# Second attention of a fused two-layer kernel: the transposed scores, the turned maxima and the heads' normalisation are placed later within the pairs of heads

## The chip, the cores and the metric

One core of a Trainium2 chip runs the whole program as one launch. The metric is the device time of one execution in microseconds (us), as a median over several. TensorE (PE), VectorE (DVE), ScalarE (ACT), GpSimd (POOL) and the queue of transfers (SP) each run their own instruction stream and meet only at semaphores.

## The reference, cut to what matters

The program computes two transformer layers on four sequences of 512 tokens and width 256. Only the second layer's attention is touched:

```python
q = (x @ Wq).reshape(b, s, 16, 16); k = ...; v = ...   # 16 heads of width 16
scores = einsum('bqhd,bkhd->bhqk', q, k) * 0.25
p = softmax(scores)
o = einsum('bhqk,bkhd->bqhd', p, v).reshape(b, s, e)
x = x + o @ Wo + bo
```

The feed-forward part that comes before it (mixture of experts) and the one after it (ternary weights, GELU) are not changed, but the second attention overlaps with both at its ends.

## The kernel before, in words

`TT` is 4 (tiles of 128 tokens), `BATCHES` 4, `PAIRS` 8: the 16 heads go through in pairs. `pair_step(b, n, ...)` is written once for each engine. It has 8 **places** `i` = 0 to 7, and in each place every engine does its share of several pairs at different stages. The order in each engine's stream is fixed by these places, written out by hand:

- *Scores.* At place `i` TensorE computes scores of pair `n`: head `h = i // 4`, query tile `t = i % 4`, 512 keys (line 1689, called S1 below). The two heads of a pair are stacked in `qst` and `kst`: head 0 in the upper 64 partitions, head 1 in the lower 64 (`rows = slice(64 * h, 64 * h + 64)`). VectorE takes the negative maximum over keys of each (line 1005) into `nm1`. There are three PSUM banks for these scores.
- *Turned maxima.* When all eight maxima of a pair are there, TensorE transposes them (line 1714, four matmuls against `ident`, into PSUM bank 7) at place 1 of the next pair, and VectorE adds them to the queries (line 1014, `qsm`).
- *Transposed scores.* TensorE computes scores with keys on the partitions (line 1702, called ST below) from `kst` and `qsm`, eight per pair, numbered `e` = 0 to 7, with head `e // 4`. They begin at place 4 of the next pair and end at place 3 of the one after it. ScalarE takes the exponential of each (line 1338) into `pT1`. There are two PSUM banks for them, so ST number `e` waits for exponential `e - 2`.
- *Values.* Two pairs together are multiplied with `v1` (line 1728, four 32-column tiles side by side; the trace shows two records for each matmul, eight in one place), at places 5 and 7 of odd pairs and 1 and 3 of even ones. ScalarE copies the sum to `oT1` at place 4 of an even pair, TensorE turns it back (line 1742, PSUM bank 7) at place 6.
- *Normalisation of the heads.* VectorE divides by the sums (lines 1032 and 1034, reciprocal and `otok`) at place 7 of the even pair, right after that place's maximum. The turned maxima of an odd pair go into the same PSUM bank 7 and wait for it (`o1_normed`), and so does the turning of `otok` (line 1640) that feeds the output projection (line 1647).

At set places TensorE also does 128-row work of other stages: projections of queries and keys (lines 1416 to 1418, places (n, i) = (0, 5), (1, 3), (4, 5), (5, 3)), of values ((2, 5), (3, 0)), transposes in pairs 3 and 4 (line 1640 at (3, 2) and (3, 4), line 1634), and the output projection at (6, 5) and (7, 3). After such a projection ScalarE has two copies to make (lines 1278 and 1324). Sequence 0 lacks the projections of (0, 5), (1, 3), (2, 5), (3, 0) and all of the output projection; the last one lacks those of (4, 5) and (5, 3).

The queue SP loads the stacked heads, ring of four (`STACK_RING`): the load for pair `k` waits until the last ST of pair `k - 4` is done (line 422), and between pairs 3 and 4 and after pair 7 it also moves the projected heads through DRAM (line 413).

After the last sequence come four pair steps without new scores (`TAIL1`), which are interleaved with the first steps of the last feed-forward: VectorE makes ternary weights after steps 0 and 1 (lines 1043 to 1055), and hidden block `f` = 0 comes after step 2, blocks 1 to 8 after step 3:

```python
MLP_AFTER = {2: (0,), 3: (1, 2, 3, 4, 5, 6, 7, 8)}
for n in range(TAIL1):
    pair_step(BATCHES, n, False, True, False)
    ...
    for f in MLP_AFTER.get(n, ()):
        mlp_step(0, f, True, False, True)
```

In `mlp_step(0, 0)` TensorE computes block 0 (line 1837), ScalarE its GELU (line 1390) and a copy (line 1395), and VectorE waits for that copy and subtracts (line 1097). In tail step 3 TensorE turns `otok` at places 0 and 2 (line 1640) and ScalarE keeps it (line 1349).

Of the kernel before, what the change touches and what calls it, by code (L numbers as in the profile page):

```python
# [23 lines left out]
TT = SEQ // P  # L24
# [52 lines left out]
def build(nc, dram, out):  # L77
    with ExitStack() as ctx:
# [261 lines left out]

        MLP_AFTER = {2: (0,), 3: (1, 2, 3, 4, 5, 6, 7, 8)}
        TAIL1 = 4
        hidden_used = lambda f: -1 if f == 0 else f - 2 if f >= 2 else None
        hidden_split = lambda f: f if f < HT else None
        hidden_age = lambda f: 2 if f < 2 else 3
# [304 lines left out]
        def _(dve):  # L650
# [343 lines left out]
            def pair_step(b, n, new, old, following, places=range(2 * TT)):  # L994

                kb, kq, i_next = b * PAIRS, b * (PAIRS // 2), b + BATCHES + 1
                valid = lambda m: new if m >= 0 else old
                for i in places:
                    if new:

                        p = 2 * TT * n + i
                        h, t = i // TT, i % TT
                        dve.wait_ge(s1_ready, kb * 2 * TT + p + 1)
                        col = 64 * h + MAX_ROW
                        V.tensor_reduce(nm1[:, n % 2, t, col:col + 1], ps[:, 1 + s1_slot(p), :], AX.X, ALU.max,  # L1005
                                        negate=True).then_inc(s1_max, 1)
                    if i == 1 and valid(n - 1):

                        m = n - 1
                        k = kb + m  # L1010
                        dve.wait_ge(m_turned, k + 1)
                        if old or m >= 2:
                            dve.wait_ge(st_ready, (k - 1) * 2 * TT)
                        V.tensor_tensor(qsm[:, m % 2, :], ps[:, 7, :], qst[:, m % STACK_RING, :], ALU.add
                                        ).then_inc(qsm_ready, 1)
                    if new and n == 1 and i % 2 == 1:

                        if i == 1:
                            if not following:
                                dve.wait_ge(raw_used, raw_before(2))  # L1020
                            dve.wait_ge(xn_ready, i_next * TT)
                            V.memset(spare[:, 1:2], 0.0)
                        norm_stats(i_next, (b + 1) % BATCHES, (i // 2,))
                    if i == 2 * TT - 1 and n % 2 == 0 and valid((n - 4) // 2):

                        u = (n - 4) // 2
                        c0 = (u % (PAIRS // 2)) * 4 * HD1
                        if u == 0 and old:
                            dve.wait_ge(on_turned, KT * b)
                        dve.wait_ge(o1_turned, kq + u + 1)  # L1030
                        o4 = ps[:, 7, :].rearrange("p (t h c) -> p t h c", t=TT, h=4)
                        V.reciprocal(oinv[:, u % 2, :, :], o4[:, :, :, HD1]).then_inc(o1_inv, 1)
                        dve.wait_ge(o1_inv, kq + u + 1)
                        V.tensor_tensor(otok[:, :, c0:c0 + 4 * HD1].rearrange("p t (h c) -> p t h c", h=4),
                                        o4[:, :, :, 0:HD1], oinv[:, u % 2, :, :].unsqueeze(3).to_broadcast((P, TT, 4, HD1)),
                                        ALU.mult).then_inc(o1_normed, 1)
# [27 lines left out]
            for n in range(1, PAIRS):  # L1064
                pair_step(0, n, True, False, True)
                if n >= PAIRS - 2:

                    i = n - (PAIRS - 2)
# [32 lines left out]

            for n in range(TAIL1):
                pair_step(BATCHES, n, False, True, False)
# [17 lines left out]
        def _(act):  # L1121
# [204 lines left out]
            def pair_step(b, n, new, old, following):  # L1326
                kb, kq = b * PAIRS, b * (PAIRS // 2)
                valid = lambda m: new if m >= 0 else old
                for i in range(2 * TT):
                    m = n - 1 if i >= TT else n - 2  # L1330
                    if valid(m):

                        e = (i - TT) % (2 * TT)
                        h, c, u = e // TT, e % TT, m // 2
                        if e == 0 and m % 2 == 0 and (old or m >= 4):
                            act.wait_ge(o1_ready, kq + u - 1)
                        act.wait_ge(st_ready, (kb + m) * 2 * TT + e + 1)
                        A(pT1[:, u % 2, 2 * (m % 2) + h, c, :], ps[:, 4 + e % 2, :], ACT.Exp, scale=SCALE1  # L1338
                          ).then_inc(p1_ready, 1)
                    if new and old and (n, i) in ((0, 5), (1, 3)):  # L1340
                        split_tile(b, 1, n, 0, old)
                        keep_raw(b, n)
                    if new and old and (n, i) in ((2, 5), (3, 0)):
                        keep_values(b, n - 2, old)
                    if old and (n, i) in (((3, 2), (3, 4)) if new else ((3, 0), (3, 2))):

                        c = i // 2 - 1 if new else i // 2
                        act.wait_ge(on_turned, KT * b - 1 + c)
                        A(oTn[:, c, :], ps[:, 0, :], ACT.Copy).then_inc(oTn_ready, 1)
                    if new and (n, i) in ((3, 6), (4, 0)):  # L1350

                        j, c = b + BATCHES + 1, n - 3
                        act.wait_ge(xn_turned, j * KT + c + 2)
                        A(xnT[0][:, c, :], ps[:, 0, :], ACT.Copy).then_inc(xnT_high, 1)
                        keep_raw(b, 2 + c)
                    if following and (n, i) in ((4, 5), (5, 3)):
                        split_tile(b + 1, 0, n - 4)
                        keep_raw(b, n)
                    if old and (n, i) in (((6, 5), (7, 3)) if new else ((3, 4), (3, 6))):

                        half = n - 6 if new else i // 2 - 2
                        act.wait_ge(out1_ready, 2 * b - 1 + half)
                        keep_raw(b, half if not new else 6 + half if following else 4 + half)
                    if n % 2 == 0 and i == 4 and valid((n - 4) // 2):

                        u = (n - 4) // 2
                        act.wait_ge(o1_ready, kq + u + 1)
                        if old or u >= 2:
                            act.wait_ge(o1_turned, kq + u - 1)
                        A(oT1[:, u % 2, :], ps[:, 6, :], ACT.Copy).then_inc(oT1_kept, 1)  # L1370
# [27 lines left out]

            for n in range(TAIL1):
                pair_step(BATCHES, n, False, True, False)  # L1400
# [10 lines left out]
        def _(pe):  # L1411
# [264 lines left out]
            def pair_step(b, n, new, old, following, places=range(2 * TT)):  # L1676
                kb, kq, i_next, before = b * PAIRS, b * (PAIRS // 2), b + BATCHES + 1, raw_before(b)
                valid = lambda m: new if m >= 0 else old
                for i in places:
                    if new:  # L1680
# [6 lines left out]
                        if old or p >= s1_age(p):  # L1687
                            pe.wait_ge(s1_max, kb * 2 * TT + p - s1_age(p) + 1)
                        MM(ps[:, 1 + s1_slot(p), :], qst[rows, n % STACK_RING, t * P:(t + 1) * P],  # L1689
                           kst[rows, n % STACK_RING, :], start=True, stop=True).then_inc(s1_ready, 1)  # L1690
                    m = n - 1 if i >= TT else n - 2
                    if valid(m):

                        e = (i - TT) % (2 * TT)
                        k = kb + m
                        h, c = e // TT, e % TT
                        rows = slice(64 * h, 64 * h + 64)
                        if e == 0:
                            pe.wait_ge(qsm_ready, k + 1)
                        if old or m >= 1 or e >= 2:  # L1700
                            pe.wait_ge(p1_ready, k * 2 * TT + e - 1)
                        MM(ps[:, 4 + e % 2, :], kst[rows, m % STACK_RING, c * P:(c + 1) * P], qsm[rows, m % 2, :],  # L1702
                           start=True, stop=True).then_inc(st_ready, 1)
                    if i == 1 and valid(n - 1):

                        m = n - 1
                        k = kb + m
                        pe.wait_ge(s1_max, (k + 1) * 2 * TT)
                        if old or m >= 1:
                            pe.wait_ge(qsm_ready, k)  # L1710
                        if n % 2 == 1 and valid((n - 5) // 2):
                            pe.wait_ge(o1_normed, kq + (n - 5) // 2 + 1)
                        for t in range(TT):
                            ins = T(ps[:, 7, t * P:(t + 1) * P], nm1[:, m % 2, t, :], ident[:])  # L1714
                        ins.then_inc(m_turned, 1)
                    u = (n - 3) // 2 if n % 2 else (n - 4) // 2
# [16 lines left out]
                    if n % 2 == 0 and valid((n - 4) // 2) and i == 6:  # L1733

                        u = (n - 4) // 2
# [106 lines left out]

            for n in range(TAIL1):
                pair_step(BATCHES, n, False, True, False)
# [89 lines left out]
```

## Time and profile before

| | |
|---|---|
| median of 3 runs | 1405.19 us (1402.77 to 1406.04) |
| the profiled execution | 1407.15 us, its span 1405.4 us |
| busy in the span: PE, PEld, DVE, ACT, POOL | 1348.3, 1071.8, 1059.2, 729.2, 477.2 us |
| second attention | from 1047.9 to about 1333 us |
| mean granted TensorE clock | 0.975 |

PE is the matmul record, PEld the weight load beside it. A matmul's record is a latency: they overlap, so the pace of TensorE is read from the distance between starts. A time is in us from the span's start. The granted clock is 1.00 at 2.4 GHz and 0.50 at 1.2 GHz.

### The profile page before, as it was taken

What the parts mean: (1) busy time and instruction counts of PE and PEld (TensorE: products, weight loads), DVE (VectorE), ACT (ScalarE), POOL (GpSimd) and SP (SyncE); (2) the same over time, 40 slices, a digit from 0 to 9 for tenths busy, and PEclk for the clock granted to TensorE, in tenths of its full rate; (3) what the DMA queues carried; (4) which work ended last, traced back from release to release, by engine and by line L of the source; (5) the groups of instructions that cost most, each with busy time, mean ns of one, the idle gap of its engine ahead of it and who ended that gap; (6) DMA issues with size and microseconds to landing.
All of it is one profiled execution on the core that took longest, in us unless ns stands there. A gap on an engine that the chain in (4) does not pass through costs nothing.

```text
span 1405.4 us, 25530 instructions
## 1 busy us (share of the span) xinstructions
PE 1348.3 (96%) x8050; PEld 1071.8 (76%) x8050; DVE 1059.2 (75%) x2468; ACT 729.2 (52%) x1899; POOL 477.2 (34%) x728
## 2 busy tenths in 40 slices
PE   5799999999999999899999999999999999999898
PEld 3588988988899889778888888888874344444487
DVE  6889999989999999667755455554658877777475
ACT  4775565556555655444432232232326676766465
POOL 5766657765776576300000000000003031331031
PEclk9999999999999999989999999999997899999899
DMA  5200000000000000055411211112253333331001
GB/s 179 83 37 1 2 1 2 2 3 1 1 1 1 1 1 1 4 156 154 142 40 61 68 40 64 62 42 93 66 173 106 107 120 121 117 120 65 0 17 44
DMA packets 45892, 80.92 MB, mean 58 GB/s; under 512 B 5608, under 2 KB 13928, under 8 KB 45484
## 3 DMA queue, kind: packets, MB, share of 16 engines
q1 hardware_dynamic: 45484, 79.35, 17.6%
q8 instruction: 60, 0.98, 0.3%
q14 instruction: 60, 0.49, 0.1%
q0 software_dynamic: 288, 0.10, 0.1%
HBM read 64.70 MB, written 15.87 MB: 57 GB/s over the span
## 4 chain that ended last, share of the span: by engine, by line
PE 68%; DVE 13%; issue 4%; POOL 3%; ACT 2%; DMA 0%; DVEq 0%; SPq 0%; ACTq 0%; POOLq 0%
PE ps L1416 13%; PE ps L1418 13%; PE ps L1417 13%; PE ps L1689 6%; PE ps L1728 5%; PE ps L1503 3%; PE ps L1459 3%; DVE ssum L805 2%; PE ps L1814 2%; DVE qkn L794 2%; PE ps L1837 2%; DVE yT L769 2%; PE ps L1702 1%; PE ps L1714 1%; POOL rope L534 1%
## 5 line engine op out<-in xcount | busy, mean ns | idle before, releaser
L1005 DVE TENSOR_REDUCE nm<-ps 128x1 f32<-128x512 f32 x256 | 166.3, 684 | 53.5 <-PE ps L1689 53.0
L1338 ACT ACTIVATE pT<-ps 128x512 f32<-128x512 f32 x256 | 143.2, 598 | 68.3 <-PE ps L1702 66.7
L1416 PE MATMUL ps<-xnT_lo,w1moe_hi 128*128 128x512 f32 x400 | 160.5, 401 | 0.2 <-DVE sg L919 0.2
L493 POOL TENSOR_TENSOR ln_rs<-ln_ve,minus_half 128x4 f32<-128x4 f32 x12 | 15.1, 1260 | 425.7 <-DVE ln_ve L666 425.7
L1418 PE MATMUL ps<-xnT_hi,w1moe_hi 128*128 128x512 f32 x400 | 159.3, 398 | 0.0
L1417 PE MATMUL ps<-xnT_hi,w1moe_lo 128*128 128x512 f32 x400 | 159.2, 398 | 0.0
L919 DVE TENSOR_TENSOR sg<-ps,sg 128x512 f32<-128x512 f32 x100 | 69.0, 690 | 113.9 <-ACT sg L1266 113.7
L1249 ACT ACTIVATE moe_act_hi<-sg 128x512 fp32r<-128x512 f32 x100 | 63.2, 632 | 151.3 <-DVE sg L929 147.4
L1416 PE MATMUL ps<-wqkv_lo,xnT_hi 128*128 128x512 f32 x256 | 127.2, 497 | 7.3 <-DVE wqkv_lo L718 3.1
L534 POOL TENSOR_TENSOR rope<-rope 128x384 f32<-128x384 f32 x128 | 132.6, 1036 | 0.0
L1266 ACT ACTIVATE sg<-ps 128x512 f32<-128x512 f32 x100 | 59.6, 596 | 123.3 <-PE ps L1418 123.3
L1503 PE MATMUL ps<-qkT 128*128 128x128 f32 x896 | 121.2, 275 | 0.0
L933 DVE TENSOR_TENSOR moe_act_lo<-sg,moe_act_hi 128x512 fp32r<-128x512 f32 x100 | 69.1, 691 | 64.5 <-ACT moe_act_hi L1249 64.5
L1702 PE MATMUL ps<-qsm,kst 64*128 64x512 f32 x256 | 113.3, 499 | 3.1 <-ACT pT L1338 2.9
L1416 PE MATMUL ps<-w2moe_lo,moe_act_hi 128*128 128x256 f32 x400 | 113.5, 284 | 0.6 <-DVE moe_act_lo L933 0.6
L532 POOL TENSOR_TENSOR rms<-msq,minus_half 128x3 f32<-128x3 f32 x128 | 110.4, 863 | 10.0
L1418 PE MATMUL ps<-w2moe_hi,moe_act_hi 128*128 128x256 f32 x400 | 112.3, 281 | 0.0
L1417 PE MATMUL ps<-w2moe_hi,moe_act_lo 128*128 128x256 f32 x400 | 112.0, 280 | 0.0
L1503 PEld LDWEIGHTS ps<-qkT 128*128 128x128 f32 x896 | 110.4, 192 | 0.5
L1689 PE MATMUL ps<-kst,qst 64*128 64x512 f32 x256 | 106.7, 490 | 3.3 <-DVE nm L1005 3.1
L1160 ACT ACTIVATE probT<-ps 128x256 f32<-128x256 f32 x128 | 49.2, 384 | 112.4 <-PE ps L1459 57.0
L1208 ACT ACTIVATE yT<-ps,nmax 128x128 f32<-128x128 f32 x256 | 92.4, 374 | 27.1 <-DVE nmax L785 26.9
(202 smaller groups left out, 3748.1 us busy)
## 6 DMA issues: line engine op xcount, KB each, us to landing
c_rows<-comb_rows SPq DMA_DIRECT2D x36, 256.0 KB, 3.3
copies<-qk_hi SPq DMA_DIRECT2D x32, 256.0 KB
qst<-copies SPq DMA_DIRECT2D x32, 256.0 KB, 2.6
kst<-copies SPq DMA_DIRECT2D x32, 256.0 KB, 3.0
yT<-in_w1moe SPq DMA_DIRECT2D x25, 256.0 KB, 2.6
x_res<-in_wqkv SPq DMA_DIRECT2D x8, 512.0 KB, 4.4
copies<-qk_lo SPq DMA_DIRECT2D x16, 256.0 KB
c_rows<-comb_rows SPq DMA_DIRECT2D x16, 224.0 KB, 3.1
```

Source lines behind the costliest of these rows:

```text
L532: nc.gpsimd.tensor_tensor(rms[:, s, :], msq[:, s, :], minus_half[:, 0:3], ALU.pow).then_inc(rms_ready, 1)
L534: nc.gpsimd.tensor_tensor(rope1[:, s, :], rope1[:, s, :], rope2[:, s, :], ALU.add).then_inc(rotated, 1)
L1005: V.tensor_reduce(nm1[:, n % 2, t, col:col + 1], ps[:, 1 + s1_slot(p), :], AX.X, ALU.max, negate=True).then_inc(s1_max, 1)
L1208: ins = A(prob[:, m % PROB_RING, h, :], ps[:, 3 + s, (2 * h + 1) * P:(2 * h + 2) * P], ACT.Exp, bias=nmax[:, s, h:h + 1], accum_out=psums[ ...
L1338: A(pT1[:, u % 2, 2 * (m % 2) + h, c, :], ps[:, 4 + e % 2, :], ACT.Exp, scale=SCALE1).then_inc(p1_ready, 1)
L1416: MM(out, left[0], right[1], start=first, stop=False, skip_group_check=True)
L1417: MM(out, left[1], right[0], start=False, stop=False, skip_group_check=True)
L1418: return MM(out, left[0], right[0], start=False, stop=last, skip_group_check=True)
L1503: ins = MM(bank[:, h, part, :], qkT[:, m % K_RING, h, :], qkT[:, (m if part else m - GROUPS) % K_RING, 2, :], start=not alone(m) and h == ...
L1689: MM(ps[:, 1 + s1_slot(p), :], qst[rows, n % STACK_RING, t * P:(t + 1) * P], kst[rows, n % STACK_RING, :], start=True, stop=True).then_inc ...
L1702: MM(ps[:, 4 + e % 2, :], kst[rows, m % STACK_RING, c * P:(c + 1) * P], qsm[rows, m % 2, :], start=True, stop=True).then_inc(st_ready, 1)
L1728: ins = MM(ps[VW * h:VW * (h + 1), 6, :], v1[:, c, col:col + VW], pT1[:, u % 2, h, c, :], start=c == 0, stop=c == TT - 1, tile_position=(0 ...
```

## The change

Three placements move, on every engine that takes part in them, and no instruction is added or removed:

- the transposed scores and their exponentials start at place 6 instead of 4 (and end at place 5 of the pair after instead of 3);
- the turned maxima and `qsm` go from place 1 to place 3;
- the normalisation of the heads goes from place 7 of an even pair to place 0 of the odd pair behind it, again right after that place's maximum.

```diff
         MLP_AFTER = {2: (0,), 3: (1, 2, 3, 4, 5, 6, 7, 8)}
         TAIL1 = 4
+        ST_AT, TURN_AT = 6, 3
...
-                    if i == 1 and valid(n - 1):
+                    if i == TURN_AT and valid(n - 1):
 
                         m = n - 1
                         k = kb + m
...
-                    if i == 2 * TT - 1 and n % 2 == 0 and valid((n - 4) // 2):
-
-                        u = (n - 4) // 2
+                    if i == 0 and n % 2 == 1 and valid((n - 5) // 2):
+
+                        u = (n - 5) // 2
                         c0 = (u % (PAIRS // 2)) * 4 * HD1
                         if u == 0 and old:
                             dve.wait_ge(on_turned, KT * b)
...
                 for i in range(2 * TT):
-                    m = n - 1 if i >= TT else n - 2
+                    m = n - 1 if i >= ST_AT else n - 2
                     if valid(m):
 
-                        e = (i - TT) % (2 * TT)
+                        e = (i - ST_AT) % (2 * TT)
                         h, c, u = e // TT, e % TT, m // 2
                         if e == 0 and m % 2 == 0 and (old or m >= 4):
                             act.wait_ge(o1_ready, kq + u - 1)
...
-                    m = n - 1 if i >= TT else n - 2
+                    m = n - 1 if i >= ST_AT else n - 2
                     if valid(m):
 
-                        e = (i - TT) % (2 * TT)
+                        e = (i - ST_AT) % (2 * TT)
                         k = kb + m
                         h, c = e // TT, e % TT
                         rows = slice(64 * h, 64 * h + 64)
...
-                    if i == 1 and valid(n - 1):
+                    if i == TURN_AT and valid(n - 1):
 
                         m = n - 1
                         k = kb + m
```

The first and second hunks are shared names and VectorE, the fourth is ScalarE, the last two are TensorE.

## Rows read from the trace of the kernel before

**Rows 1.** The page: busy time of TensorE, and the chain by line.
```profile
PE 1348.3 (96%) x8050; PEld 1071.8 (76%) x8050; DVE 1059.2 (75%) x2468; ACT 729.2 (52%) x1899; POOL 477.2 (34%) x728
...
PE ps L1416 13%; PE ps L1418 13%; PE ps L1417 13%; PE ps L1689 6%; PE ps L1728 5%; PE ps L1503 3%; PE ps L1459 3%; DVE ssum L805 2%; PE ps L1814 2%; DVE qkn L794 2%; PE ps L1837 2%; DVE yT L769 2%; PE ps L1702 1%; PE ps L1714 1%; POOL rope L534 1%
```

**Rows 2.** Busy by stretch: PE, PEld, DVE, ACT, POOL (instructions), clock, DMA share, GB/s.
```profile
1054.60:1075.10 20.50, 19.73 (x60) 9.73 (x59) 18.18 (x38) 11.06 (x19) 9.58 (x7) 0.50 0.18 56
...
1102.40:1112.70 10.30, 9.30 (x34) 3.11 (x36) 8.62 (x11) 3.70 (x7) 0.00 (x0) 0.50 0.29 98
...
1177.30:1242.00 64.70, 63.57 (x388) 30.89 (x384) 50.17 (x92) 45.92 (x86) 18.57 (x14) 1.00 0.35 114
...
1283.30:1290.20 6.90, 6.83 (x28) 2.92 (x32) 4.69 (x8) 2.96 (x6) 0.00 (x0) 0.51 0.26 95
```

**Rows 3.** Timeline of PE, third sequence, pair 0 from place 4: start, us, instruction.
```profile
1181.18 0.49 PE L1689 MATMUL ps<-kst,qst 64*128 64x512 f32 x1
...
1181.18 0.49 PE L1702 MATMUL ps<-qsm,kst 64*128 64x512 f32 x1
...
1181.51 0.39 PE L1689 MATMUL ps<-kst,qst 64*128 64x512 f32 x1
1181.52 0.39 PE L1702 MATMUL ps<-qsm,kst 64*128 64x512 f32 x1
...
1181.84 0.50 PE L1416 MATMUL ps<-xnT_lo,wqk_hi 128*128 128x512 f32 x1
...
1182.17 0.40 PE L1417 MATMUL ps<-xnT_hi,wqk_lo 128*128 128x512 f32 x1
```

**Rows 4.** Timeline of PE: first two, then three scores on the same half.
```profile
1047.87 0.74 PE L1689 MATMUL ps<-kst,qst 64*128 64x512 f32 x2
...
1047.87 0.97 PE L1689 MATMUL ps<-kst,qst 64*128 64x512 f32 x3
```

**Rows 5.** Timeline of PE at half clock, first sequence, pair 3, places 3 and 4.
```profile
1071.33 0.62 PE L1689 MATMUL ps<-kst,qst 64*128 64x512 f32 x1
...
1071.76 0.62 PE L1689 MATMUL ps<-kst,qst 64*128 64x512 f32 x1
```

**Rows 6.** Timeline, third sequence, from place 7 of pair 0 to place 3 of pair 1.
```profile
1184.45 0.50 PE L1689 MATMUL ps<-kst,qst 64*128 64x512 f32 x1
...
1184.51 2.29 ACT L1338 ACTIVATE pT<-ps 128x512 f32<-128x512 f32 x4
...
1185.60 0.25 DVE L1032 RECIPROCAL oinv<-ps 128x16 f32<-128x16 f32 x1
...
1185.88 0.42 DVE L1034 TENSOR_TENSOR otok<-ps,oinv 128x256 f32<-128x256 f32 x1
...
1186.45 0.63 PE L1714 MATMUL ps<-ident,nm 128*128 128x128 f32 x4 [0.28 <-DVE otok L1034]
...
1187.67 0.50 PE L1416 MATMUL ps<-xnT_lo,wqk_hi 128*128 128x512 f32 x1
```

**Rows 7.** Timeline of the same pair 1, values at places 5 and 7.
```profile
1189.93 1.07 PE L1728 MATMUL ps<-pT,v 128*32 128x512 f32 x8
...
1191.92 1.07 PE L1728 MATMUL ps<-pT,v 128*32 128x512 f32 x8
```

**Rows 8.** Timeline: the load for pair 4 is issued, and pair 4 begins.
```profile
1200.72 0.43 SPq L425 DMA_DIRECT2D kst<-copies  x1
...
1209.58 0.49 PE L1689 MATMUL ps<-kst,qst 64*128 64x512 f32 x1
```

**Rows 9.** The page: issue to landing of that load, in us.
```profile
kst<-copies SPq DMA_DIRECT2D x32, 256.0 KB, 3.0
```

**Rows 10.** Timeline of the tail: last values, both turns of `otok`, VectorE's subtraction.
```profile
1316.64 5.72 PE L1728 MATMUL ps<-pT,v 128*32 128x512 f32 x32
...
1324.56 0.66 PE L1640 MATMUL ps<-ident,otok 128*128 128x128 f32 x4
...
1326.10 0.69 DVE L1097 TENSOR_TENSOR hact_lo<-hact,hact_hi 128x512 fp32r<-128x512 f32 x1 [1.60 <-ACT hact_hi L1395]
1326.61 0.42 PEld L1640 LDWEIGHTS ps<-ident,otok 128*128 128x128 f32 x4 [1.63 <-ACT oTn L1349]
```

## Prediction

> **What bounds the kernel now.** The page comes first: TensorE is busy 96% of the span, and the costliest lines of the chain are its own [rows 1]. A matmul's record is a latency, so that alone proves little. The busy times by stretch come next: in a whole sequence of the second attention at full clock (64.7 us, 8.1 a pair) TensorE shows 63.6, VectorE 50.2 and ScalarE 45.9 us [rows 2]. Then the timeline of TensorE by starts. At places 4 and 5 a score and a transposed score start within 0.01 us of each other, and the next two follow 0.33 us later, and after another 0.33 the projection begins [rows 3]. A stream of full-width 512-column matmuls behind one another costs 0.23 each: the first score's record is 0.50 long, the next 0.39, so 0.11 is the weight load that nothing covers, and 0.33 + 0.33 is 0.20 for entering and leaving the mode plus 2 x 0.23. So a **couple (S1 and ST) costs one stream of 0.23, not two**: they run side by side. The code says why they can: S1 of place i uses head i // 4, ST uses head e // 4 with e = i - 4, so always the other 64 partitions.
>
> Where does TensorE wait? At each odd pair 1, 5 and 7. From place 7 of pair 0 to the turned maxima it takes 1186.45 - 1184.45 = 2.0 us for three couples, which alone cost 0.20 + 3 x 0.23 = 0.9: 1.1 us of waiting [rows 6]. Some of it is ScalarE, late by its two copies after the projection: four exponentials follow in 2.29 us, 0.57 each, and every ST waits for the exponential two before it. The rest is the normalisation that holds bank 7 (0.28 us named). A second wait is at places 6 and 7 of pairs 1 and 5: values to values take 1.99 us, of which 1.00 is the values and 0.66 two couples, so 0.33 [rows 7, 3]. Elsewhere in a full pair TensorE has no gap. In short pairs without 128-row projections, VectorE is as full as TensorE: 18.2 of 20.5 us at half clock [rows 2].
>
> **The change, part by part.**
>
> *Transposed scores from place 6.* Now e = i - 6 modulo 8. Place 0 and 1: ST of head 0 (e = 2, 3) beside S1 of head 0. Places 2, 3: ST of head 1, S1 of head 0. Places 4, 5: ST of head 1 (e = 6, 7) beside S1 of head 1. Places 6, 7: ST of head 0 beside S1 of head 1. So in **four of eight places both matmuls want the same 64 partitions**. No such couple is in the trace; the price is bounded. From above and likeliest: rows of scores alone on one half, two of them 0.74 us, three 0.97, so each further one costs 0.23 even there [rows 4], its load covered. From below: nothing, were they still side by side. I take 0.23, since the scores without a partner are the same instruction on the same half. Pairs with S1 and a same-half ST: 6 in the first sequence (pairs 2 to 7), 24 in the others, 30 x 4 = 120 couples, x 0.233 = **+28.0**. About 12 of these lie at half clock (pairs 2 and 3 of the first sequence, places 4 and 5 of two pairs later [rows 2]), where a stream on one half costs 0.43 [rows 5]: 12 x 0.2 = **+2.3**.
>
> The Trainium skill bears on this ("TensorE: Matmul & The Clock Gate", Part 3, What overlaps and what doesn't): a weight load overlaps matmuls in flight only where the row group differs. By that rule each same-half matmul would pay its 0.11 load too, 120 x 0.11 = 13 more, and by the row it doesn't: three scores on one half step by 0.23. The trace disagrees, and the sum goes by the trace; the rule is kept as a rival.
>
> *What waiting covers.* Pairs 1, 5, 7 (2 in the first sequence, 9 in the others, 11). Places 0 to 3 are now contiguous, with turned maxima behind them. ST at place 0 still starts at 1185.17 on this timeline (exponential 1 of four ended), the next at 1185.68; then places 2 and 3 at ScalarE's pace, 1186.31 and 1186.88; turned maxima at 1187.3, 0.56 to 0.59 long, so the projection starts at about 1187.9 instead of 1187.67 [rows 6]. That is +0.22 where the two same-half couples would cost 0.47: covered 0.25 x 11 = **-2.7**. The normalisation, now one maximum (0.64) later, ends at about 1187.0, before the maxima want bank 7: that wait is gone, but ScalarE's pace eats what it gives. The wait of 0.33 at places 6 and 7 goes in 6 full-clock pairs, because TensorE arrives there later: **-2.0**. Pair 3 saves 0.1 in three sequences: **-0.3**. Short pairs: those of the first sequence take 20.5/3 = 6.8 us at half clock; TensorE's own streams become 4 x 0.43 + 4 x 0.86 and about 1.1 us for the maxima with 0.4 of entering, 6.7, so they grow little, I say 0.3 each instead of 1.7. With four later short pairs, which wait about 0.4 each at place 6, I take **-4.4** (nothing covered: 0; all: -7).
>
> *Maxima at place 3.* Four transposes as before. Behind them VectorE's addition (place 3, behind that place's maximum), behind that the maxima of places 4 and up. ST number 0 wants it at place 6: three places, as before. Bank 7 is wanted by the turn of `oT1` at place 6 of even pairs, three places on instead of five, over 2 us: covered. In even pairs the values already break the couples at places 1 and 3, so no mode change is added.
>
> *Transfers.* Every load of a ring slot waits for ST number 7, two places later, and SP issues in order, so the moves through DRAM behind the load for pair 3 start about 3 us later too. The load for pair 4 is issued at 1200.72 and lands 3.0 later; pair 4 begins at 1209.58: 5.9 us of slack, less 3, plus what TensorE itself is later: covered [rows 8, 9]. VectorE's and POOL's inputs are unchanged.
>
> *The tail.* Here no score accompanies the ST, and two more of the last pair's eight come after step 0; each takes ScalarE's 0.57 or more, so the last values begin 1.2 us later than 1316.64: **+1.2**. And VectorE's normalisation of the last pairs moves from step 2 to step 3, **behind hidden block 0**, that is behind the subtraction that waits for GELU and copy. It ends at 1326.79; the normalisation takes 0.70 (1185.60 to 1186.30); so the first turn of `otok` starts at 1327.55 instead of 1324.56. The second, which waited for ScalarE until 1326.61, then comes at about 1328.77, being 1.2 behind the first (a turn to its last transpose, ScalarE's copy): **+2.2** [rows 6, 10]. Queued behind TensorE's wait are the output projection and blocks 1 to 8, so it reaches the end. The early normalisation now also precedes the second ternary tensor by 0.7 us; that is needed only after the last values: covered.
>
> Sum: 28.0 + 2.3 - 2.7 - 2.0 - 0.3 - 4.4 + 1.2 + 2.2 = **+24.3 us**. Against the profiled span, 1405.4 + 24.3 = 1429.7; the profiled execution was 1407.15, the median of the runs 1405.19, so in the median 1429.5.
>
> **The rivals.**
>
> *R1, the load is not covered* between two matmuls of the same half, because S1 and ST alternate: the uncovered load of 0.11 (0.50 less 0.39) comes on top, 120 x 0.11 = 13 [rows 3]. For it: S1 and ST read two different stationary tensors, scores in a row read one. Against: each of those scores loads its own weights too, at a step of 0.23. 1429.5 + 13 = 1442. It is what the rule of the Trainium skill's page above would do here.
>
> *R2, the halves don't matter*: the same-half couple still costs one stream. Against: the row of scores alone steps by 0.23. Left are ScalarE's pace, 11 x 0.2, and the tail, 3.4: +5.6, 1411.
>
> *R3, faster*: halves don't matter, and the 1.1 us before the turned maxima are the fault of bank 7, not of ScalarE, so they go in 11 pairs: -12 + 3.4 = -8.7, 1396.5. Against: only 0.28 of the wait is VectorE's by name. It decides as soon as a same-half couple costs under 8.7/120 = 0.07 us more.
>
> *R4, the clock*: the half-clock stretches of 10.3 and 6.9 us [rows 2] each follow short pairs in which TensorE waits. Denser work may keep it at full clock there (about -4), or a longer wait in the tail may bring another (+3). That moves the forecast inside its range.
>
> **How the numbers follow.** Forecast (with R4 inside it) 0.78, its own range 1421 to 1436; R1 0.07; R2 0.08; R3 0.04; 0.03 for no change by some mixture. The range of 8 in 10 takes a little to both sides: 1418 to 1438. A measurement of this kernel tells 0.2% (2.8 us) from no change. Faster 0.04, same 0.03, slower 0.93.
>
> **What would show it.** At places 0, 1, 4 and 5 S1 and ST start 0.23 us apart instead of together, and two such places span 1.1 us to the next 128-row work, not 0.66. A full-clock sequence grows from 64.7 to about 70.6 us. VectorE's idle time before its maxima grows; the maxima never wait for `otok`. The first turn of `otok` in the tail waits for VectorE some 3 us. I am wrong if same-half starts stay together (R2), if they are 0.33 or more apart (R1), or if places 0 to 3 of odd pairs end earlier than now (R3).

## The result and the profile after

The changed kernel takes **1428.95 us** (median of 4 runs, 1427.98 to 1431.53) against 1405.62 for the kernel before: ratio 1.0174, 95% interval 1.0158 to 1.0189, so 1.7% slower. Beside other kernels on one chip (below) it was 1.0183 (1.0165 to 1.0201). The profiled execution took 1428.68 us with a span of 1426.9, 21.5 us longer than before.

The page of the changed kernel, busy time and the chain by line (S1 is now line 1690, ST line 1703, everything behind the first hunk one line lower). Against [rows 1], TensorE has 23 us more of busy time with the same 8050 matmuls (its weight loads 18 us more), and VectorE, ScalarE and GpSimd are within 2 us of before:

```profile
PE 1371.4 (96%) x8050; PEld 1090.2 (76%) x8050; DVE 1058.7 (74%) x2468; ACT 731.0 (51%) x1899; POOL 477.7 (33%) x728
...
PE ps L1417 13%; PE ps L1419 13%; PE ps L1418 13%; PE ps L1690 6%; PE ps L1729 5%; PE ps L1703 4%; PE ps L1504 3%; PE ps L1460 3%; PE ps L1815 2%; DVE ssum L806 2%; DVE qkn L795 2%; PE ps L1838 2%; PE ps L1715 1%; DVE yT L770 1%; DVE nmax L786 1%
```

Busy by stretch in the changed kernel, columns as in [rows 2]: the half-clock stretch in the first sequence, then the third sequence, then pairs 4 and 5 of the last:

```profile
1052.50:1079.80 27.30, 26.72 (x75) 13.88 (x76) 20.05 (x40) 12.90 (x21) 11.08 (x8) 0.50 0.26 81
...
1186.90:1256.90 70.00, 69.95 (x389) 35.47 (x385) 50.21 (x92) 46.32 (x87) 18.57 (x14) 1.00 0.32 106
1292.10:1306.90 14.80, 14.67 (x84) 6.65 (x80) 11.73 (x20) 10.43 (x20) 2.43 (x2) 1.00 0.25 79
```

A sequence at full clock went from 64.7 to 70.0 us; TensorE is now busy for 69.95 of the 70.00, VectorE does the same 50.2 as before. The half-clock stretch grew from 20.5 to 27.3 us, while the one at 1283 us [rows 2], inside pairs 4 and 5 of the last sequence, has no counterpart.

What TensorE does in places 0 and 1 of an even pair (timeline of PE, third sequence, pair 2):

```profile
1203.63 0.49 PE L1690 MATMUL ps<-kst,qst 64*128 64x512 f32 x1
1203.96 0.39 PE L1703 MATMUL ps<-qsm,kst 64*128 64x512 f32 x1
1204.20 0.39 PE L1690 MATMUL ps<-kst,qst 64*128 64x512 f32 x1
1204.43 0.39 PE L1703 MATMUL ps<-qsm,kst 64*128 64x512 f32 x1
1204.76 0.64 PE L1729 MATMUL ps<-pT,v 128*32 128x512 f32 x4
```

In [rows 3] the two of a place started together. Here each starts behind the last: the second 0.33 after the first, which holds the 0.11 of entering the 64-row work once, the others 0.24 and 0.23 on. Two places span 1204.76 - 1203.63 = 1.13 us instead of 0.66.

Where the time lies, by the starts of S1. The sequences of the kernel before begin at 1047.87, 1112.39, 1177.26 and 1242.02 and the last score starts at 1305.78; those of the changed kernel (timeline of PE, first scores, and the last):

```profile
1045.97 0.74 PE L1690 MATMUL ps<-kst,qst 64*128 64x512 f32 x2
...
1116.77 0.72 PE L1690 MATMUL ps<-kst,qst 64*128 64x512 f32 x1
...
1186.94 0.49 PE L1690 MATMUL ps<-kst,qst 64*128 64x512 f32 x1
...
1256.90 0.49 PE L1690 MATMUL ps<-kst,qst 64*128 64x512 f32 x1
...
1322.95 0.39 PE L1690 MATMUL ps<-kst,qst 64*128 64x512 f32 x1
```

| stretch | before | after | difference |
|---|---|---|---|
| sequence 1 | 64.5 | 70.8 | +6.3 |
| sequence 2 | 64.9 | 70.2 | +5.3 |
| sequence 3 | 64.8 | 70.0 | +5.2 |
| sequence 4, to its last score | 63.8 | 66.1 | +2.3 |
| last score to the end of the span | 99.6 | 103.9 | +4.3 |

That is +23.4; the attention happened to begin 1.9 us earlier in this execution, which leaves the span's 21.5.

The odd pair (timeline of the changed kernel, third sequence, from place 7 of pair 0; compare [rows 6]):

```profile
1195.03 0.50 PE L1690 MATMUL ps<-kst,qst 64*128 64x512 f32 x1
...
1197.06 0.42 DVE L1035 TENSOR_TENSOR otok<-ps,oinv 128x256 f32<-128x256 f32 x1
...
1197.43 0.50 PE L1703 MATMUL ps<-qsm,kst 64*128 64x512 f32 x1
1197.86 0.66 PE L1715 MATMUL ps<-ident,nm 128*128 128x128 f32 x4
1198.27 0.48 PE L1417 MATMUL ps<-xnT_lo,wqk_hi 128*128 128x512 f32 x1
```

From place 7 to the projection: 3.24 us, against 3.22 before. The turned maxima wait for nothing now, but they come after four places and not after two.

The tail (timeline of the changed kernel; compare [rows 10]):

```profile
1335.05 5.65 PE L1729 MATMUL ps<-pT,v 128*32 128x512 f32 x32
...
1344.43 0.69 DVE L1098 TENSOR_TENSOR hact_lo<-hact,hact_hi 128x512 fp32r<-128x512 f32 x1 [4.81 <-ACT hact_hi L1396]
...
1345.32 0.42 DVE L1035 TENSOR_TENSOR otok<-ps,oinv 128x256 f32<-128x256 f32 x1
...
1345.80 1.00 PE L1641 MATMUL ps<-ident,otok 128*128 128x128 f32 x4 [2.79 <-DVE otok L1035]
```

VectorE divides only after the subtraction of hidden block 0, and TensorE stands 2.79 us for it.

### The profile page after: what moved, and what is told of

Read it like the earlier page. It is cut to its first block, busy times and chain, and to the rows that moved or that the text cites. A ratio compares the mean times of both kernels' runs of the same rounds, so it can differ in the third digit from the quotient of the medians.

```text
span 1426.9 us, 25530 instructions
## 1 busy us (share of the span) xinstructions
PE 1371.4 (96%) x8050; PEld 1090.2 (76%) x8050; DVE 1058.7 (74%) x2468; ACT 731.0 (51%) x1899; POOL 477.7 (33%) x728
## 4 chain that ended last, share of the span: by engine, by line
PE 71%; DVE 12%; issue 4%; POOL 3%; ACT 2%; DMA 0%; DVEq 0%; SPq 0%; ACTq 0%; POOLq 0%
PE ps L1417 13%; PE ps L1419 13%; PE ps L1418 13%; PE ps L1690 6%; PE ps L1729 5%; PE ps L1703 4%; PE ps L1504 3%; PE ps L1460 3%; PE ps L1815 2%; DVE ssum L806 2%; DVE qkn L795 2%; PE ps L1838 2%; PE ps L1715 1%; DVE yT L770 1%; DVE nmax L786 1%
## 5 line engine op out<-in xcount | busy, mean ns | idle before, releaser
L1690 PE MATMUL ps<-kst,qst 64*128 64x512 f32 x256 | 113.4, 479 | 4.2 <-DVE nm L1006 3.9
```

## The experiments

Ratios and differences are to the kernel before on the same chip (median 1403.90 us beside E1 to E4, 1403.54 beside E5 to E8, 1404.35 beside E9 and E10).

**E1, halves apart.** The changed kernel, with another order of the scores of a pair on VectorE and on TensorE, and nothing else:

```diff
+        S1_ORDER = ((1, 0), (1, 1), (0, 0), (0, 1), (0, 2), (0, 3), (1, 2), (1, 3))
...
-                        h, t = i // TT, i % TT
+                        h, t = S1_ORDER[i]
```

> The changed kernel with the scores of a pair in another order: places 0 and 1 take two tiles of head 1, places 2 to 5 the four of head 0, places 6 and 7 the other two of head 1, so that S1 is always on the other 64 partitions than ST. All three placements stay as changed. Theory (same-half couples are two streams): S1 and ST start together in every place, and what is left over the kernel before is ScalarE's pace (2.2 us) and the tail (3.4 us), some +5.6, so 1411 us, 18 us under the changed kernel. Rival (the loss comes from the placements themselves, waits that they bring): it stays near 1429 us.

Measured 1406.58 us, ratio 1.0020 (1.0008 to 1.0031): +2.7. Of the 1.74% only 0.2% are left, with all three placements as changed. That is 3 us less than the expected +5.6; its odd pairs take 8.14 us against 8.12 before, so the 2.2 us set down for ScalarE's pace were not there. Timeline of PE of this kernel, third sequence, pair 2, places 0 and 1, the same work as in the fence above:

```profile
1191.83 0.50 PE L1691 MATMUL ps<-kst,qst 64*128 64x512 f32 x1
1191.83 0.50 PE L1704 MATMUL ps<-qsm,kst 64*128 64x512 f32 x1
1192.17 0.39 PE L1691 MATMUL ps<-kst,qst 64*128 64x512 f32 x1
1192.17 0.39 PE L1704 MATMUL ps<-qsm,kst 64*128 64x512 f32 x1
1192.49 1.07 PE L1730 MATMUL ps<-pT,v 128*32 128x512 f32 x8
```

The couples start together again and two take 0.66. A full-clock sequence takes 64.9 us. What is left lies in the tail: from the last score to the end this trace takes 102.8 us, the kernel before 99.6. So nearly all of the loss is the sharing of the 64 partitions, and not the distance between stages. Whether TensorE's rows or the memory behind the same 64 partitions set the price, no run here tells apart.

**E2, all eight on one half.** The kernel before, its placements untouched:

```diff
+        S1_ORDER = ((1, 0), (1, 1), (1, 2), (1, 3), (0, 0), (0, 1), (0, 2), (0, 3))
...
-                        h, t = i // TT, i % TT
+                        h, t = S1_ORDER[i]
```

> The kernel before with its placements untouched and only the order of the scores reversed by heads (head 1 first), so that S1 and ST want the same 64 partitions in all eight places, 8 a pair instead of 0 (and 4 in the change). Theory: 244 same-half couples at 0.233 us are 57 us, of which the waits of the kernel before (1.1 us in 11 odd pairs, 0.33 in 6, and those of the short pairs) cover some 12 to 18: +39 to +45, 1445 to 1451 us. Rival (halves don't matter): 1405 us.

Measured 1456.55 us (four runs, 1446.98 to 1464.23), ratio 1.0369 (1.0311 to 1.0427): +52.6, above the expected 39 to 45. Busy by stretch: two half-clock stretches and the third sequence:

```profile
1051.30:1095.70 44.40, 43.33 (x119) 21.25 (x120) 26.00 (x48) 19.41 (x33) 13.15 (x9) 0.50 0.24 83
1119.60:1140.10 20.50, 20.50 (x61) 8.54 (x61) 10.60 (x14) 6.36 (x12) 0.00 (x0) 0.50 0.17 52
1208.60:1284.40 75.80, 74.69 (x388) 38.69 (x384) 50.61 (x91) 46.69 (x86) 18.55 (x14) 1.00 0.29 97
```

At full clock a sequence takes 75.8 us: +11.0 for 64 couples, against +5.2 for 32 in the changed kernel. The price follows the number of couples, about 0.17 each after what waits cover (0.233 gross would be 14.9). Four such sequences would be +44, as expected. What goes beyond it lies in the first two sequences (81.3 and 81.7 us), which hold the half-clock stretches of 44.4 and 20.5 us; the kernel before had 20.5 and 10.3.

**E3, only the normalisation moved** (the kernel before with the third hunk of the diff alone).

> The kernel before with only the normalisation moved, from place 7 of even pairs to place 0 of odd ones. The turned maxima stay at place 1 of the odd pair and wait for it on bank 7. Theory: the normalisation ends one maximum (0.64 us) later, 11 times 0.65 is 7, and the tail pays 2.2 for standing behind hidden block 0: +9, 1414.5 us. Rival (ScalarE alone sets the pace there, and the tail is hidden): within 2 us of before.

Measured 1417.17 us (1413.1 to 1420.29), ratio 1.0102 (1.0071 to 1.0133): +13.3, somewhat above the +9; the profiled execution took 1414.63. Timeline of its third sequence, pair 1:

```profile
1189.28 0.42 DVE L1034 TENSOR_TENSOR otok<-ps,oinv 128x256 f32<-128x256 f32 x1
...
1189.85 0.63 PE L1714 MATMUL ps<-ident,nm 128*128 128x128 f32 x4 [0.88 <-DVE otok L1034]
```

The named wait is 0.88 instead of 0.28, pair 1 takes 8.71 instead of 8.12. And the tail's first turn of `otok` waits 2.8 us. In this trace a full-clock sequence takes 66.6 us instead of 64.8: its three odd pairs are each 0.6 longer. So the normalisation at place 0 is a loss by itself as long as the turned maxima want bank 7 at place 1; moved together they don't meet.

**E4, the tail's normalisation early.** The changed kernel, with the old place in the four tail steps:

```diff
-                    if i == 0 and n % 2 == 1 and valid((n - 5) // 2):
+                    place, lead = (0, 5) if new else (2 * TT - 1, 4)
+                    if i == place and n % 2 == lead % 2 and valid((n - lead) // 2):
...
-                        u = (n - 5) // 2
+                        u = (n - lead) // 2
```

> The changed kernel, but in the four tail steps after the last sequence the normalisation stands at its old place 7 of the even pair, ahead of hidden block 0. Theory: the first turn of otok no longer waits for the subtraction behind GELU, and the second waits for ScalarE as before: 2.2 us less than the changed kernel, 1426.8 us. Rival (the block after the tail is bound by something else, so the wait is absorbed): the changed kernel's 1429 us.

Measured 1424.76 us, ratio 1.0145 (1.0122 to 1.0169), 0.4% under the changed kernel's 1.0183 on another chip. The intervals overlap at the edge, so the time alone doesn't settle it; E7 against E1 does (below). The timeline of its tail:

```profile
1345.27 0.42 PEld L1642 LDWEIGHTS ps<-ident,otok 128*128 128x128 f32 x4 [0.31 <-DVE otok L1036]
...
1346.81 0.69 DVE L1099 TENSOR_TENSOR hact_lo<-hact,hact_hi 128x512 fp32r<-128x512 f32 x1 [1.60 <-ACT hact_hi L1397]
```

The turn now precedes the subtraction; its weight load waits 0.31 us for VectorE, and its matmul no longer stands for 2.79. From the last score to the end this trace takes 98.3 us, the changed kernel's 103.9 (102.9 in E5).

**E5, the changed kernel again,** on the chip of the next three.

> The changed kernel unaltered, beside the next three on one chip: ratio 1.0174 as in the result, some 23 to 24 us over the kernel before.

1429.24 us, ratio 1.0183. Its sequences: 68.7, 70.3, 70.0, 66.0 us.

**E6, only the transposed scores moved** (`ST_AT, TURN_AT = 6, 1`, normalisation at its old place).

> The kernel before with only the transposed scores moved, from place 4 to place 6; turned maxima and normalisation stay. Theory: the same-half couples are all there, so nearly all of the loss is: places 0 and 1 of the odd pairs hide behind the wait for the normalisation that is still there, the values of the tail come 1.2 us later, the 2.2 to 2.5 us behind hidden block 0 don't occur. A full-clock sequence takes about 70 us, the whole about +21. Rival (the other two moves help, 1 us in each of 11 odd pairs): +30 or more without them.

Measured 1424.12 us (1423.17 to 1425.04), ratio 1.0140 (1.0123 to 1.0157): +20.6 (expected +21). A full-clock sequence takes 70.0 us, exactly what it takes with all three moved. The other two moves bring nothing in the sequences and cost what stands in the tail.

**E7, both repairs**: E1 and E4 together.

> The changed kernel with both repairs, halves apart (as in the first experiment) and the tail's normalisation early (as in the fourth). Theory: the two are independent, +2.7 less 2.5 to 3: level with the kernel before, 0 +- 1.5 us. Rival (the gain of the tail was the clock's): +2.7 stays.

1400.85 us, ratio 0.9982 (0.9970 to 0.9993): 2.7 us under the kernel before, more than the expected 0 +- 1.5. The second repair is worth 0.4% here as well (1.0020 to 0.9982), and these intervals are apart. Its full-clock sequence is no shorter than before (64.9 us). Its trace spends less time at half clock: the mean granted clock is 0.985 against 0.975.

**E8, ScalarE's second copies put off,** on top of E7:

```diff
-                        keep_raw(b, n)
+                    if new and old and (n, i) in ((1, 1), (1, 7)):
+                        keep_raw(b, i // 4)
```

and in the same way (5, 1), (5, 7) and (7, 1), (7, 7).

> The same with one more edit: ScalarE's second copy behind each projection (raw, line 1324 of the kernel before) no longer comes at once but after the exponentials of the next places: (0, 5) to (1, 1), (1, 3) to (1, 7), the same in pairs 4 and 5, (6, 5) to (7, 1), (7, 3) to (7, 7). Theory: in odd pairs 1, 5 and 7 ScalarE's pace sets when the fourth transposed score starts, so one copy less before it (0.5 us) brings 0.5 in 11 pairs and some of the 0.33 wait at places 6 and 7 in 6: 5 to 7 us under the kernel before, and it becomes the fastest. Rival (something else, VectorE or the rings, holds the odd pairs): no change against the kernel without this edit.

1401.48 us, ratio 0.9982 (0.9971 to 0.9993): no gain over E7, where 5 to 7 us under the kernel before were expected. Its full-clock sequence takes 64.8 us, but not evenly: pairs 1 and 5 fell from 8.13 to 7.78 and 7.80, and pair 2 rose from 7.53 to 8.11. The timeline of pair 2, with GpSimd's subtraction beside VectorE's small step of the layer norm (line 668), which takes 0.92 us here:

```profile
1193.16 1.28 POOL L602 TENSOR_TENSOR qk_lo<-raw,qk_hi 128x512 fp32r<-128x512 f32 x1 [4.48 <-ACT raw L1327]
...
1193.55 0.92 DVE L668 TENSOR_SCALAR ln_ve<-bn_mv 128x4 f32<-128x4 f32 x1
```

**E9, only the first of the two copies put off,** the second where it was.

> Halves apart, tail early, and only the first copy of each two put off ((0, 5) to (1, 1), (4, 5) to (5, 1), (6, 5) to (7, 1)); the second stays at (1, 3), (5, 3), (7, 3). The kernel with both put off gained 0.35 us in each odd pair and lost 0.58 in pair 2, where GpSimd's subtraction for the second copy then ran beside VectorE's small step of the layer norm (0.92 us instead of 0.17). Theory: without the second the gain stays and the loss goes: a full-clock sequence takes 63.9 to 64.2 us, the whole 2 to 3.5 us under the kernel with both repairs, some 0.3 to 0.4% under the kernel before. Rival: the stall in pair 2 has another cause and stays at 0.5.

1401.07 us, ratio 0.9975 (0.9965 to 0.9985), the lowest ratio of all, but its interval overlaps E7's. Pair 2 is back at 7.48 and line 668 at 0.17 us in all three sequences, as expected. The gain in pairs 1 and 5, however, is gone too (8.12), and the full-clock sequence takes 64.9 us where 63.9 to 64.2 were expected. The gain had come from the *other* copy, the one behind the projection at place 3, and not ahead of the turned maxima: from the values at place 5 of pair 1 to those at place 7 it is 1.66 us in E8, but 2.00 in E9 and 1.98 in E7, while the first values stand at the same distance from the pair's start in all three (5.13 to 5.14). Timeline of PE, third sequence, pair 1, in E8:

```profile
1189.95 1.07 PE L1733 MATMUL ps<-pT,v 128*32 128x512 f32 x8
...
1191.61 1.06 PE L1733 MATMUL ps<-pT,v 128*32 128x512 f32 x8
```

and in E9:

```profile
1188.84 1.07 PE L1733 MATMUL ps<-pT,v 128*32 128x512 f32 x8
...
1190.84 1.07 PE L1733 MATMUL ps<-pT,v 128*32 128x512 f32 x8
```

So that copy makes the second wait of 0.33 us, and the theory that the first copy holds the turned maxima fell. Timeline of E9's third sequence, from the exponential of place 6 to the turned maxima of pair 1:

```profile
1182.95 0.59 ACT L1341 ACTIVATE pT<-ps 128x512 f32<-128x512 f32 x1
...
1183.38 0.72 PE L1707 MATMUL ps<-qsm,kst 64*128 64x512 f32 x2
...
1183.94 1.78 ACT L1341 ACTIVATE pT<-ps 128x512 f32<-128x512 f32 x3 [0.40 <-PE ps L1707]
...
1185.77 0.49 PE L1707 MATMUL ps<-qsm,kst 64*128 64x512 f32 x1
1186.19 0.66 PE L1719 MATMUL ps<-ident,nm 128*128 128x128 f32 x4
```

With one copy less ahead of it, ScalarE now *waits* 0.40 us for the ST of place 7, which TensorE can't issue before it has turned `oT1` at place 6. From that ST on: 0.56 to its exponential, three exponentials at 0.59, and the last ST of the four can start. The ring of two banks and the run of exponentials hold the odd pair; the last of the four STs comes 2.39 us after that of place 7, and in E7, with the copy at its old place, 2.40.

**E10, the same copy put off in the kernel before.**

> The kernel before with nothing but that same copy put off. Theory (two waits lie over one another in the odd pairs of the kernel before, ScalarE's pace and bank 7, held by the normalisation): taking ScalarE's away leaves the turned maxima where they are, because the normalisation still ends at the same time; pairs 1 and 5 stay within 0.1 us of 8.1 and the time within 0.2% of before. Rival (ScalarE alone): 0.35 to 0.5 less in each odd pair, some -4 us.

1404.46 us, ratio 0.9997 (0.9986 to 1.0007); pair 1 stays at 8.1. As expected, but after E9 it doesn't tell bank 7 from the ring: either alone would have held the pair.

## Why the prediction was right, point by point

Forecast 1429.5, measured 1428.95. Forecast +24.3; measured +23.3 between the medians, +21.5 between the two spans, and +23.4 from the start of the attention to the end. The cause and its place were right, and several terms were off by amounts that cancelled. That the sum came within 1 us is luck: the first sequence alone takes 68.7, 70.8, 72.4 and 73.9 us in the four traces with four same-half places (E5, the changed kernel, E6, E4).

- *Same-half couples are two streams* (+28.0): confirmed by starts 0.23 apart, by E1, which takes the sharing away and with it all but 0.2%, and by E2, which doubles it. Rival R2 (halves don't matter) and R3 (faster) are out. R1 (the weight load comes on top) is out as well: the step is 0.23 to 0.24 with S1 and ST alternating, so the load stays covered although both use one row group. The 0.33 from the first to the second, by which the forecast would have called itself wrong, comes once on entering and not at each step. The Trainium skill ("TensorE: Matmul & The Clock Gate", Part 3, What overlaps and what doesn't) states that a load overlaps matmuls in flight only when the row group differs; the step of 0.23 disagrees. The same Part names the background weight buffer as a second way for a load to go ahead; the step agrees with that.
- *Odd pairs, cover of 0.25 each*: better than forecast. The forecast put the projection 0.22 us later; it came 0.02 later. The turned maxima started as computed (2.83 us after place 7, forecast 2.85), but with a projection of the same tile shape right behind they take 0.41 us, not 0.56 to 0.59. The forecast had named ScalarE's two copies and its pace together; E9 shows that ahead of the turned maxima only the pace holds.
- *The second wait of 0.33 goes*: right, in the third sequence the values of pair 1 start at 1200.97 and 1202.63, 1.66 apart instead of 1.99. By E8 and E9 this wait is made by ScalarE's second copy.
- *A full-clock sequence 70.6 us*: 70.0. The missing 0.6 are the three odd pairs, each about 0.2 shorter than forecast.
- *Short pairs grow by only 0.3 each* (-4.4 in all): mis-sized. In the half-clock stretch pair 2 grew from 6.8 to 8.7 us and pair 3 from 9.6 to 12.6. In E1, with the halves apart and a half-clock stretch of 20.5 us, they take 7.2 and 9.8: most of the growth is the sharing. The argument counted TensorE's streams in a pair (6.7 us) against 6.8 and took the engines' waits for each other as free. The timeline of PE in places 4 to 6 of pair 2 shows streams end to end, a start every 0.43 us:

```profile
1064.31 0.62 PE L1703 MATMUL ps<-qsm,kst 64*128 64x512 f32 x1
1064.74 0.62 PE L1690 MATMUL ps<-kst,qst 64*128 64x512 f32 x1
1065.16 0.62 PE L1703 MATMUL ps<-qsm,kst 64*128 64x512 f32 x1
1065.59 0.62 PE L1690 MATMUL ps<-kst,qst 64*128 64x512 f32 x1
```

  VectorE, which was to be the cover, is busy 20.05 of 27.3 us there, against 18.18 of 20.5 [rows 2]. And the stretch itself lasted 6.8 us longer, which the forecast had priced only for the tail. Pair 1 of that sequence, on the other hand, fell from 7.0 to 6.0 us, which no term had. The first sequence is +6.3, about twice what its terms gave (some 3.2).
- *R4, the clock, inside the forecast*: it went both ways at once. The stretch at 1283 us vanished and pair 5 of the last sequence took 6.9 us instead of 9.4, which is why the last sequence shows +2.3 and not +5. This paid for the first sequence. Both the longer first stretch and the missing later one are in part chance of the execution. In E5 the first stretch was 23.9 us and the first sequence 68.7. And E10, with TensorE's order as in the kernel before, has no half-clock stretch in its last sequence, which takes 61.4 us instead of 63.8.
- *The tail*: values +1.2 (measured 12.09 us behind the last score, 10.87 before), first turn of `otok` 2.84 later (forecast 2.99), second turn 2.5 later (forecast 2.2), each against the values. Shown by E4 and E3 too. By the ratios of E1 and E7 the repair is worth 5 us, more than the 3 by which the first turn comes earlier (10.2 us behind the values in E1, 7.3 in E7). The traces show the rest behind it, in the granted clock. Where the normalisation stands behind hidden block 0 (the changed kernel, E1, E3, E5), 6.8 us at half clock begin within 0.6 us of the first turn, and from that turn to the end it is 80.9 to 81.1 us. In E4 and E6 to E9 no such stretch follows, and it is 79.2 to 79.3. But the kernel before and E10 have 3.4 us at half clock a little behind the turn and 80.8, and E2 has 6.8 and 82.2, so the early place alone doesn't keep the clock up. No term of the sum held this; the forecast had it only in R4.
- *Maxima, transfers*: in sequences 2 and 3 of the changed kernel the waits of TensorE's matmuls are an empty list, and its weight loads wait for maxima and exponentials only, never for `qsm` or a transfer, as said. The time by itself of "maxima at place 3" was never measured alone; E6 says that together with the normalisation it is worth nothing.

## What to carry to other kernels

Before moving a stage by a few places, list which part of TensorE's array each matmul uses beside its new neighbours: two matmuls of 64 rows run as one stream only on different halves, and here half the couples on the same half cost 5.2 us of 65. If the move is wanted, reorder the other stage by the same amount (E1 did it with a table of eight entries). And where a loop's last steps are interleaved with the next stage, read the engine's order there by itself: a place that is free inside the loop stood behind a GELU in the tail.

## What the runs showed of the hardware that was not expected

- A weight load for the same half of the array was covered by the running matmul (0.23 us a step, at half clock 0.43), in an alternation of two different stationary tensors.
- In E8 a four-element-wide VectorE `tensor_scalar` took 0.92, 0.92 and 0.98 us instead of 0.17 in the three sequences in which a GpSimd subtraction of 512 columns (1.28 us) had begun 0.3 to 0.4 us before; both ended together (1194.47 and 1194.44). Put apart in time (E9), it took 0.17. The Trainium skill, "SBUF — State Buffer", "SBUF: two separate sides", states that GpSimd and a VectorE instruction in a two-port mode, or with two inputs in SBUF, share a pair of ports by an exclusive lock for a whole instruction. The trace agrees in that the later one waits for the end of the earlier one; in which mode the `tensor_scalar` ran, no trace shows.
- The first half-clock stretch tends to be longer with more same-half couples, but varies by the execution: 20.5 or 23.9 us with none (seven traces), 23.9, 27.3, 30.7 and 34.1 with four of eight places (E5, the changed kernel, E6, E4), 44.4 with all eight (one trace), although TensorE's matmul records are the same in number. Ahead of the first of these stretches TensorE had been busy for only 4.55 of 6.70 us (kernel before, 1047.9 to 1054.6). Why the stretch gets longer is not settled here.
